# Graph network of four layers: the first layer's symmetric scores computed once, the adjacency turned afterwards

## The reference, cut to what matters

```python
# layer 0
node_att = softmax(x @ node_w, axis=0)
h = x @ edge_w
e = h @ h.T                               # symmetric: e[i, j] == e[j, i]
e = where(adj > 0, e, NEG_BIG)
edge_att = softmax(e, axis=1)
x = layernorm(x + adj * (node_att * edge_att) @ (x @ weight) + bias)
# layer 1
h = x @ W_sa;  e = where(adj != 0, exp(-leaky_relu(s_left[:, None] + s_right[None, :])), 0)
x_a = (e / e.sum(1)) @ h;  x_b = adj @ (x @ W_gcnb) + b_gcnb
x = layernorm(x + sigmoid(attn_a * x_a + attn_b * x_b))
# layers 2 and 3 use adj from its turned copy too
```

## Time and profile before

| | |
|---|---|
| median of 3 runs | 816.06 us |
| the 3 runs | 812.24, 816.06, 821.02 us |
| the profiled execution's own time | 812.18 us |
| its span in the trace | 810.4 us |
| mean granted clock | 0.995 of full |
| PE / DVE / ACT / POOL busy in the span | 770.1 / 448.3 / 330.9 / 98.9 us |
| end of layer 0's last weighted sum | 227.4 us |

### The profile page before, as it was taken

How to read it: one execution, slowest core, us unless ns; L and a number is a source line. 1 busy time by engine, 2 the same in 40 slices (tenths; PEclk the granted TensorE clock), 3 DMA queues, 4 the chain that set the end, 5 groups by cost and what they waited for, 6 DMA issues and landing times.

```text
span 810.4 us, 11790 instructions
## 1 busy us (share of the span) xinstructions
PE 770.1 (95%) x4288; PEld 509.5 (63%) x4288; DVE 448.3 (55%) x933; ACT 330.9 (41%) x496; POOL 98.9 (12%) x203
## 2 busy tenths in 40 slices
PE   6988998999999999999979999999999999999997
PEld 5765666666677878786835554755765456465443
DVE  3576767678859788888873357220243311114465
ACT  3565455457467555555541133321343222224000
POOL 1011122101230010100111121000000100000343
PEclk9999998999999999999999999999999999999999
DMA  8969999997500000000002000000000000000011
GB/s 220 184 112 184 178 182 177 176 191 133 106 7 14 1 1 1 1 1 2 0 25 61 0 1 0 1 0 0 0 1 26 1 1 0 0 0 1 15 45 45
DMA packets 112571, 42.41 MB, mean 52 GB/s; under 512 B 103312, under 2 KB 109584, under 8 KB 112528
## 3 DMA queue, kind: packets, MB, share of 16 engines
q1 hardware_dynamic: 110224, 33.44, 21.0%
q0 software_dynamic: 2304, 8.39, 6.6%
HBM read 22.95 MB, written 2.10 MB: 31 GB/s over the span
## 4 chain that ended last, share of the span: by engine, by line
PE 58%; issue 24%; DVE 5%; SPq 4%; ACT 4%; DMA 3%; POOL 2%; POOLq 0%; ACTq 0%; DVEq 0%
PE ps L665 11%; PE ps L816 10%; PE ps L794 8%; PE ps L576 5%; PE ps L588 4%; PE ps L851 4%; PE ps L825 3%; SPq L377 3%; PE ps L777 3%; PE ps L590 2%; DMA turned<-pl 2%; PE ps L535 2%; PE ps L841 2%; PE ps L558 2%; POOL rstd L429 1%
## 5 line engine op out<-in xcount | busy, mean ns | idle before, releaser
L665 PE MATMUL ps<-adjT,x 128*128 128x512 bf16 (+1 forms) x768 | 174.6, 380 | 6.8 <-DVE x L1431 4.3
L665 PEld LDWEIGHTS ps<-adjT,x 128*128 128x128 f16 x768 | 71.7, 98 | 90.3 <-issue 5.9
L1149 DVE TENSOR_TENSOR hh_lo<-hf,hh_hi 128x512 fp32r<-128x512 f32 x32 | 22.2, 692 | 134.5 <-ACT hf L1085 133.4
L588 PE MATMUL ps<-sup,turned 128*128 128x512 f16 x256 | 84.1, 380 | 2.7 <-DMA turned<-pl 2.4
L816 PE MATMUL ps<-adjT,G 128*128 x384 | 83.6, 379 | 0.4 <-ACT hf L1085 0.4
L714 PE MATMUL ps<-H_hi,es_hi 128*128 128x258 f32 x256 | 76.7, 300 | 2.5 <-DVE es_lo L1149 2.2
L714 PE MATMUL ps<-H_hi,es_lo 128*128 128x258 f32 x256 | 72.4, 283 | 0.0
L714 PE MATMUL ps<-H_lo,es_hi 128*128 128x258 f32 x256 | 72.4, 283 | 0.0
L590 PE MATMUL ps<-sup,turned 128*128 128x256 f16 x256 | 69.8, 273 | 0.0
L816 PEld LDWEIGHTS ps<-adjT,G 128*128 128x128 f16 x384 | 37.2, 98 | 45.4 <-issue 0.9
L1200 DVE SCALAR_TENSOR_TENSOR pl<-em,ph 128x1024 f16<-128x1024 f32 x32 | 40.8, 1314 | 36.8 <-DMA turned<-pl 30.9
(11 more groups left out here) (208 smaller groups left out, 1437.7 us busy)
## 6 DMA issues: line engine op xcount, KB each, us to landing
adjb<-in_adj POOLq DMA_DIRECT2D x16, 512.0 KB, 7.0
x<-in_x SPq DMA_DIRECT2D x4, 512.0 KB, 7.7
out<-adjf SPq DMA_DIRECT2D x16, 128.0 KB, 1.7
adjf<-in_L_gnn_W SPq DMA_DIRECT2D x1, 1024.0 KB, 6.1
W1f<-in_L_gnn_W SPq DMA_DIRECT2D x1, 512.0 KB, 3.7
adjf<-in_L_gnn_W SPq DMA_DIRECT2D x1, 512.0 KB, 3.9
we<-in_L_gnn_edge_w SPq DMA_DIRECT2D x1, 256.0 KB, 3.8
w0x<-in_L_gnn_weight SPq DMA_DIRECT2D x1, 256.0 KB, 7.0
```

The source lines that it names most:

```text
L588: ins = mm(bank(6 + u), PT(HI, u)[:, jt, :], sup[:, jt, :], start=(jt == 0), stop=False, skip_group_check=True)
L665: ins = mm(bank(4 + f), x16[:, part, jt, f * P:(f + 1) * P], adj(b, jt), start=(jt == 0 and part == HI), stop=(jt == T - 1 and part == LO))
L1149: return tt(to, frm, high.bitcast(F32), ALU.subtract)
```

## The change

`MIRROR = 2`. From row 2 on, ScalarE copies each row's scores right of its own tile from PSUM into `kept` (91 blocks of 128 x 128 f32, placed where the blocks 1 to 3 of `adjT` will be; `keep_row`, 28 copies, put ahead of `exp_row(t)`). From row 4 on, `scores(t)` fills the tiles 2 to t - 1 by TensorE transposes of kept blocks (one 128 x 128 f32 transpose each) and computes only the tiles 0 and 1 (256 columns) and those from its own on; in the last row of a group of four it starts one tile earlier, so that no product is narrower than 256 columns. `masked_max` now waits as well until the copies out of its banks are done. Row tiles 0 to 3 of the adjacency are turned at the start as before; the other twelve are loaded a second time into two buffers in `adjf`'s room and turned after the last scores: row 4 between the turned parts of the rows 14 and 15, row 5 after row 15, and 6 to 15 during layer 1's blocks 0 and 1, with GpSimd's loads in its program ahead of `norm_factor` of these blocks. The largest weight is spread over partitions by a TensorE transpose (after `scores(6)`) and a VectorE maximum, in place of GpSimd's all-reduce, and `weight_parts` comes after round 7 instead of 6. Waits on the landed `adjT` change with this.

```diff
+    MIRROR = 2
+        kept = sb(before, "kept", [P, sum(T - 1 - t for t in range(MIRROR, T - 1)), P])
...
             for t in range(T):
                 turn_p(t, HI)
                 turn_p(t, LO)
-                if t + AB < T:
-                    turn_adj(t + AB)
+                if t == T - 2:
+                    sp.wait_ge(e_mm, B * T)
+                    turn_later(TB)
+            for t in (TB + 1,):
+                turn_later(t)
...
+            for t in range(TB + 2, T):
+                turn_later(t)
...
             def load_adj(t):
                 if t >= AB:
-                    pool.wait_ge(adjT_landed[t % AB], 16 * (t // AB))
+                    if t < AB + TB:
+                        pool.wait_ge(adjT_landed[t % AB], 16)
                     pool.wait_ge(fill_ready, t - AB + 1)
...
+            def load_later(t):
+                k = ROW_AT[t]
+                if t == TB:
+                    pool.wait_ge(w16_ready, 1)
+                elif rows_at(k, t) == 1:
+                    pool.wait_ge(p1_mm, TURNS)
+                    pool.wait_ge(w_ready, 2)
+                else:
+                    pool.wait_ge(row_turned[k], 16 * (rows_at(k, t) - 1))
+                nc.gpsimd.dma_start(rowb[k], adj_in[t * P:(t + 1) * P, :]).then_inc(row_landed[k], 16)
...
-                if t == 2:
-                    pool.wait_ge(wsmax_ready, 1)
-                    nc.gpsimd.partition_all_reduce(gw[:, 1:2], gw[:, 0:1], P, RMAX).then_inc(wsmax_all, 1)
+                if t in LATER_LOADED:
+                    load_later(LATER_LOADED[t])
...
+                if t == T - 3:
+                    load_later(TB + 1)
...
-            with pool.Fori(0, B) as b:
-                own.enter(b, TB)
+            for b in range(B):
+                for t in range(TB + 2, 3 * TB) if b == 0 else range(3 * TB, T) if b == 1 else ():
+                    load_later(t)
                 for k in range(TB):
                     norm_factor(T + b * TB + k, k % 2)
...
             def scores(t):
+                own = t - (t % TB == TB - 1) if t >= TB else 0
+                wait_from(pe, s_kept, banks_kept(t, -1))
                 for c in range(B):
                     if c % 2 == 0:
                         wait_from(pe, e_read, 2 * (t - 1) + c // 2 + 1)
-                    for k in range(KD):
...
+                    for m in range(max(MIRROR, TB * c), min(own, TB * c + TB)):
+                        ins = nc.tensor.transpose(ps[:, c, (m - TB * c) * P:(m - TB * c + 1) * P],
+                                                  kept[:, kept_at(m, t), :], ident[:, :])
+                    for first, last in ((0, MIRROR if own else 0), (own, T)):
+                        first, last = max(first, TB * c), min(last, TB * c + TB)
+                        if first >= last:
+                            continue
+                        for k in range(KD):
+                            for p, q in ((HI, HI), (HI, LO), (LO, HI)):
+                                ins = mm(ps[:, c, (first - TB * c) * P:(last - TB * c) * P],
+                                         hT[p][:, k, t * P:(t + 1) * P], hT[q][:, k, first * P:last * P],
+                                         start=(k == 0 and (p, q) == (HI, HI)), stop=(k == KD - 1 and p == LO))
+                    ins.then_inc(e_mm, 1)
...
+                if t == 6:
+                    pe.wait_ge(wsmax_ready, 1)
+                    nc.tensor.transpose(bank(4, P), gw[:, 0:1].to_broadcast([P, P]), ident[:, :]).then_inc(wsmax_all, 1)
...
+            def keep_row(t):
+                for c in kept_banks(t):
+                    first = max(TB * c, t + 1)
+                    act.wait_ge(e_mm, B * t + c + 1)
+                    run(kept[:, kept_at(t, first):kept_at(t, TB * c + TB), :].rearrange("p a b -> p (a b)"),
+                        ps[:, c, (first - TB * c) * P:CB], ACT.Copy).then_inc(s_kept, 1)
...
             for t in range(2, T):
+                keep_row(t)
                 exp_row(t)
...
             def masked_max(t, u, h):
-                dve.wait_ge(e_mm, 2 * t + h + 1)
+                dve.wait_ge(e_mm, B * t + 2 * h + 2)
+                wait_from(dve, s_kept, banks_kept(t, 2 * h + 1))
...
                 dve.wait_ge(wsmax_all, 1)
+                own.link(nc.vector.reduce_max(gw[:, 1:2], bank(4, P), AX_X))
...
-                if t == 6:
+                if t == 7:
                     weight_parts()
```

More of the change, by code:

```diff
@@ L136, in build @@
         supf = sb(before, "supf", [P, T, D])
+        before.close()
+        before = ExitStack()
+        sb(before, "first_block_2", [P, T, CB], BF16)
+        kept = sb(before, "kept", [P, sum(T - 1 - t for t in range(MIRROR, T - 1)), P])
         before.close()
@@ L172, in in_room, with rows_at @@
             return flat.rearrange("p (a b) -> p a b", a=shape[0]) if len(shape) == 2 else flat
[L174 to L178, removed]
+        wgx = in_room(0, KD, D + 2)
+        scr = in_room(KD * (D + 2), D)
+        w16 = in_room(KD * (D + 2), KD * (D + 4)).bitcast(F16).rearrange("p (a k n) -> p a k n", a=2, k=KD)
+        wsx = in_room(ROOM_B, KD, D + 4)
+        arow = in_room(ROOM_B + KD * (D + 4), 2 * D)
+        rowb = [in_room(first, N // 2).bitcast(BF16) for first in (ROOM_B, 0)]
+        ROW_AT = {t: t % 2 if t >= 2 * TB else 0 for t in range(TB, T)}
+        def rows_at(k, last):
+            return sum(ROW_AT[t] == k for t in range(TB, last + 1))
         wlf = in_room(0, KD, D)
@@ L211, in build, with kept_at, kept_banks, banks_kept @@
         lay0.close()
+        def kept_at(t, c):
+            return sum(T - 1 - r for r in range(MIRROR, t)) + c - t - 1
+        def kept_banks(t):
+            return range((t + 1) // TB, B) if MIRROR <= t < T - 1 else ()
+        def banks_kept(t, last):
+            return sum(len(kept_banks(r)) for r in range(t)) + sum(c <= last for c in kept_banks(t))
         def PT(part, u):
@@ L298, in build @@
         node_exp, node_sum = sem("node_exp"), sem("node_sum")
+        s_kept = sem("s_kept")
         e_mm, e_read, e_maxed = sem("e_mm"), sem("e_read"), sem("e_maxed")
         adjT_landed = [sem(f"adjT_landed{k}") for k in range(AB)]
+        row_landed, row_turned = ([sem(f"{name}{k}") for k in range(2)] for name in ("row_landed", "row_turned"))
         fill_ready, exp_done = sem("fill_ready"), sem("exp_done")
@@ L383, in _ @@
                 turn_p(t, LO)
-                if t + AB < T:
-                    turn_adj(t + AB)
+                if t == T - 2:
[3 more added lines that the diff above has]
+                turn_later(t)
             sp.wait_ge(xb_ready, T)
             sp.dma_start(brow[:, :], vec_row(bg_in)).then_inc(bias1_landed, 16)
-            sp.wait_ge(H_ready, 2)
+            for t in range(TB + 2, T):
+                turn_later(t)
+            for k in range(2):
+                sp.wait_ge(row_turned[k], 16 * rows_at(k, T - 1))
             sp.dma_start(wlf[:, :, :], w_tiles(wl2_in)).then_inc(wt2_landed, 16)
@@ L609, in turn16 @@
                 pe.wait_ge(conv_lo, 2 * g + 2)
+                if g == 0:
+                    pe.wait_ge(w16_ready, 1)
                 if g == 2:
@@ L728, in block1 @@
                 wait_from(pe, g_ev, b * TB)
+                if b:
+                    for k in range(2):
+                        pe.wait_ge(row_turned[k], 16 * rows_at(k, b * TB + TB - 1))
                 for pair in range(PAIRS):
@@ L921, in conv_high @@
                         act.wait_ge(fill_ready, T)
-                        for k in (0, 1):
-                            act.wait_ge(adjT_landed[k], 16 * (T // AB))
                     act.wait_ge(y_normed, t + 1)
@@ L1251, in conv_first @@
                         dve.wait_ge(fill_ready, T)
-                        for k in (2, 3):
-                            dve.wait_ge(adjT_landed[k], 16 * (T // AB))
                     dve.wait_ge(conv_hi, t + 1)
@@ L1347, in edge_scores @@
                 j0 = 2 * pair
+                if b and pair == 0:
+                    for k in range(2):
+                        dve.wait_ge(row_turned[k], 16 * rows_at(k, b * TB + TB - 1))
                 own.link(ts(nb[:, :, :], adjT[:, bass.ds(b, 1), j0:j0 + 2, :].rearrange("p a j c -> p (a j) c"), -1.0, -FAR, ALU.add, ALU.mult))
@@ L1434, in _ @@
             for k in range(AB):
[L1435 removed]
+                dve.wait_ge(adjT_landed[k], 16)
             dve.wait_ge(ex_made, 6)
```

29 lines of the change are left out of this document (12 added, 17 removed).

## The result

| | before | after |
|---|---|---|
| median in the same session | 825.06 us (6 runs, 812.24 to 835.68) | 806.09 us (6 runs, 801.55 to 808.20) |
| ratio | | 0.9888, interval 0.9841 to 0.9934 |
| the same pair in a second session | 813.88 us (19 runs, 809.72 to 826.68) | 811.20 us (10 runs, 801.99 to 817.44); ratio 0.9933, 0.9887 to 0.9979 |
| the profiled execution's own time / span | 812.18 / 810.4 us | 806.02 / 804.2 us |

The change makes the kernel about 1% faster, 5 to 9 us by the two ratios, where 13 were forecast (11.0 between the profiled executions, which show 6.2). The median lies inside the range. The ratios leave out executions more than 1.5% above the fastest of the same kernel, so they are not the quotients of the medians.

What follows compares the result with a forecast made beforehand. VectorE and ScalarE's 9.08 us loop would set the rounds: 109.0 + 1.0 + 4.7 + 2.4 + 3.0 = 120.1 against 132.1 us; less 1 for the clock, gain 11.0, giving 801.2. Forecast median 803, range 793 to 813.

Steps and rivals of the forecast that it cites:

- TensorE's prices: Scores from row 4 on, priced per product and transpose: 46.2 us against 65.9, so TensorE has 19.7 us less.
- The loop and what comes on top: VectorE and ScalarE set rounds 4 to 15: 109.0 us, plus copies 1.0, weight products and parts 4.7, conversions 2.4.
- conversions in rounds 14 and 15: Conversions between the two maxima, three tiles in each of these rounds: 1.2 us a round, 2.4 in all.
- The DMA waits: Eight rounds with an adjacency load wait for late turned parts: 0 to 9.6 us in all, 3 taken.
- the main theory: The loop of VectorE and ScalarE sets the rounds: 797 to 807 us, chance 55%.
- All-reduce: Removing GpSimd's all-reduce ends the delay in round 7, 15.4 us instead of 10.7; included in the new sum.
- Row 15's tail: Last weighted sum still begins 12.0 us after row 15's `negm`; TensorE's wait may lower the clock, 1 us taken.
- Layer 1: Twelve more loads and turnings in a stage with idle DMA, about 11 us a pair in one buffer: cost nothing.
- DMA or ScalarE stay late: Loads land late in every round (9.6 us) or copies are uncovered (6.6): gain 0 to 7, 805 to 812; 20%.
- TensorE alone counts: TensorE's 19.7 us plus round 7's 4.7 come off in full: gain 24.4, 788 us; below 797, chance 10%.
- The clock falls in the rounds: TensorE's idling in rounds lowers its clock, 3.3 us each fall; in all nine from row 7, 822 us; 7%.
- GpSimd late in layer 1: GpSimd's queue runs late from reloads in layer 1: gain 0 or less, 812 us and more; chance 5%.

Runs made afterwards that it cites:

- the best kernel: Changed kernel with two buffers each for `ph` and `pl`, `MIRROR = 4`, row 4's second load in GpSimd's round 9 or 8: 795.70 or 795.48 us.

## Why the prediction was right and wrong

**TensorE's prices: right.** Scores of row 4: 75.85 to 80.9, 5.0 us (5.1). Row 12, TensorE's timeline:

```profile
163.88 0.38 PE L630 MATMUL ps<-ident,kept 128*128 128x128 f32 x2
...
166.84 0.40 PE L638 MATMUL ps<-hT_hi,hT_lo 128*128 128x512 f32 x1
```

With the last product's pitch of 0.23 that is 3.2 us, as forecast. Switching between transposes and products costs nothing that shows.

**The loop and what comes on top: right.** Without loads in the rounds the twelve take 116.1 us; the sum without its DMA term was 109.0 + 1.0 + 4.7 + 2.4 = 117.1. Piece by piece: bare rounds 9.01 (9.08); copies 0.5 (1.0); weight products 11.51 - 9.01 = 2.5 and parts 11.49 - 9.01 = 2.5, so 5.0 (4.7); conversions in rounds 14 and 15 10.22 + 10.17 - 2 x 9.01 = 2.4 (2.4).

**The DMA waits: the step that failed.** "The eight rounds with a load then wait between 0 and 1.2 us each, 0 to 9.6 us; I take 3." Measured: 127.0 - 116.1 = 10.9 us. Of it
- 6.4 us are the mask loads (123.9 us with them, 117.5 without, row 4's load in round 9 in both). The form of the step held: against the kernel without any load, five of the rounds 4 to 11 are 0.7 to 1.7 us longer. The size was taken at half. I priced a load by its share of the DMA engines, 2.7 us behind a landing at 11.2, so 13.9 after `negm`. Row 8's low part lands 143.89 - 129.18 = 14.7 after it with one load in the way: queued beside a load, the high part takes 7.9 us instead of 4.5, and the low part is issued only when SyncE is through with the high part.
- the other 4.5 us are row 4's second load: 3.1 for its place (127.0 against 123.9) and 1.4 that it costs in round 9 as well (117.5 against 116.1). The prediction has "Twelve more loads and turnings" under layer 1, and of row 4 only the turning, in SyncE's queue. `LATER_LOADED = {5: 4}` puts its load into the rounds, next to a mask's load; it was costed nowhere. Round 10 takes 15.4 us with it in one profile and 25.4 in the other, 10.7 with it elsewhere, and moving it is worth some 6 us by the ratios of the second session. This is an instruction of a moved step that wasn't counted in the queue it was moved into.

Each of these differences is between two profiled executions.

With 10.9 us in place of 3 the sum is 128.0 and the gain 132.1 - 128.0 - 1 = 3.1 us. The profiled executions show 6.2: 1.0 more from the loop, 0.3 from the tail, 2.7 from an early row 3, and 0.9 less behind layer 0 (below). So the size of the gain is in part luck, and so is it that 806.09 lies inside 797 to 807, the span given to the main theory.

Two slips in the working leave the sum and the range as they are: the loop without DMA waits and clock gives 132.1 - 117.1 = 15.0, not 16, and by the prediction's own prices TensorE idles 0.2 us in rounds 10 and 11, and 0.7 to 1.1 only from row 12 on.

**What the gain consists of: not as told.** Of the 19.7 us less work on TensorE the prediction gave the loop's share as gain. The runs show that with the turnings and the all-reduce out of the rounds, full products reach 802.8 already. The rows of before show one half of it: the loop's 9.08 and TensorE's 10.7 are 1.6 us apart. The waits for landed parts are the other: they lengthen most rounds with a load by 0.7 to 1.7 us. While VectorE waits for a transfer, TensorE has the time that its full products need. No run puts the turnings alone back into the rounds, so their share of the gain isn't separated from the all-reduce's 3 us by a run of its own.

**The other terms.** *All-reduce:* 4.7 us inside the sum; putting it back costs 3 (3.6 in the rounds). *Row 15's tail:* the last weighted sum begins 214.91 - 202.19 = 12.7 us after `negm`, 0.7 more than forecast from before, for the 1 that was set down. *Layer 1:* GpSimd's first norm factor comes 7.1 us earlier than at 297.03, as much as the last weighted sum is earlier (222.0 to 214.9), so the twelve reloads cost nothing there (in one buffer, the reloads of layer 1's first block are 9.8 us apart, where 11 were assumed):

```profile
289.93 0.27 POOL L467 TENSOR_TENSOR rstd<-mv,epsc 128x1 f32<-128x1 f32 x1 [28.33 <-DVE mv L1240]
```

*Not in the sum:* `negm` of row 3 is 2.7 us earlier (75.22 for 77.94), and 2.4 of that is there at `negm` of row 0 already (31.81 for 34.24), before any changed instruction. The other kernels have row 0's at 31.3 to 33.5, so this is a matter of one execution; and the last stage takes 1.9 us longer, of which other stages give back 1.0. TensorE there in the changed kernel, and the window behind it (columns of the earlier trace rows):

```profile
762.16 2.31 PE L921 MATMUL ps<-x,adjT 128*128 128x512 f16 x5 [2.28 <-DVE y L1633]
...
762.00:767.00 5.00, 4.84 (x15) 1.90 (x16) 3.12 (x9) 0.00 (x0) 3.11 (x7) 0.66 0.19 63
```

In the kernel before, at the same place:

```profile
769.98 2.33 PE L851 MATMUL ps<-x,adjT 128*128 128x512 f16 x10 [1.93 <-DVE y L1553]
...
770.00:775.00 5.00, 5.00 (x24) 2.27 (x25) 4.00 (x11) 0.00 (x0) 2.92 (x7) 1.00 0.18 60
```

and in the second execution of the changed kernel:

```profile
772.97 5.35 PE L921 MATMUL ps<-x,adjT 128*128 128x512 f16 x24 [2.28 <-DVE y L1633]
...
773.00:778.00 5.00, 5.00 (x24) 2.29 (x25) 4.08 (x11) 0.00 (x0) 2.92 (x7) 1.00 0.18 61
```

After an idle time of 2.28 us the granted clock was 0.66 in the first, half speed for most of the window, and full in the other, which is the same program with the same idle time. The 160 products take 36.4 us with the fall and 34.7 without, 1.7 us. So the fall is not shown to be a property of the change.

**The rivals.** "DMA or ScalarE stay late" (20%, gain 0 to 7, 805 to 812) is what came, for its DMA half; its ScalarE half is refuted by the run without copies. "TensorE alone counts" is refuted: even the best kernel's rounds take 9.03 us. "The clock falls in the rounds" came only behind the long wait for the DMA in round 10 (granted 0.57 from 144 to 152 us), as a consequence, and in the tail (0.87 from 195 to 205, 0.79 from 205 to 215) around a wait of 4.8 us. In rows 13 to 15, with 11 or 12 transposes each, the granted clock is 1.00 from 170 to 195 us, so no cost of what the Trainium skill ("TensorE: Matmul & The Clock Gate", PE-mode transpose) says of transposes shows in these rows. "GpSimd late in layer 1" is refuted by its first norm factor.

## What to carry to other kernels

When two limits lie within 1.6 us of each other, taking away one shows nothing: here less TensorE work alone gave 1 us, a second buffer alone 0, both 7; so cost the second limit, or the pair, before believing a saving. Write down for every moved transfer in which round of which queue it is now issued and what is in flight there; here the place of a single load of 512 KB, beside another and beside a transpose, cost some 6 us where 13 were forecast for the whole change. And price a transfer by its landing beside the other queue's traffic, not by its share of the DMA engines.

## What the runs showed of the hardware

- Transposed parts (128 x 2048, f16) land in 4.5 and 4.9 us alone, 7.9 and 4.4 with one load of 512 KB beside the high part, 10.2 and 9.4 with two, and 16.9 and 19.5 in the longest round. SyncE is held by the issue meanwhile (5.4 us for the high part against 1.8 undisturbed, 10.7 for the low part at worst).
- A full DMA share doesn't say that much is moved. The longest round, in one execution and in the columns of the earlier trace rows, had 106 GB/s at a share of 1.30, where the first profile's round 10 had 218 at 1.15:

```profile
138.00:158.00 20.00, 4.13 (x30) 3.42 (x27) 3.39 (x11) 6.64 (x8) 1.99 (x4) 0.65 1.30 106
```

- Behind GpSimd's all-reduce over partitions, 0.38 us in the trace, its queue did nothing for 7.5 us more (7.2 in the kernel before).
- The length of an idle time alone did not decide whether the clock fell. In the last stage TensorE stands idle at the same place in all fourteen traces. The granted clock fell behind it in eight of them, after 2.00 to 2.33 us, and not in the other six, after 1.93 to 2.34 us. What decides, the traces don't show.
